# The routing stage of a graph and mixture-of-experts layer: ranks taken one group later on VectorE, scales ahead of picks, one load behind a store

## The chip, the cores and the metric

The kernel runs on one core of one Trainium2 chip. The metric is the device time of one execution in microseconds (us). A core has five engines that run their own instruction streams and meet at semaphores: TensorE (PE, with its weight loads shown as PEld), VectorE (DVE), ScalarE (ACT), GpSimd (POOL) and SyncE (SP), which here only issues DMAs.

## The reference

6250 nodes of 256 features, 100,000 edges, 8 experts of hidden size 1024, two of which are picked per node. Cut to what matters:

```python
xn = _layernorm(x)
x = x + gnn(xn, edges) + mix(xn)              # segment mean over edges, linear attention
# the stage that the change touches prepares this:
xt = _layernorm(x)
logits = xt @ Wr + br                         # 8 logits per node
top_p, top_idx = top_k(softmax(logits), 2)
weights = top_p / top_p.sum(-1)
h = gelu(layernorm_e(xt) @ W1[e] + b1[e]);  y = h @ W2[e] + b2[e]
out = (weights * y[top_idx]).sum(1)
x = x + out
```

## The kernel before

It has three parts in time. The first (0 to 1389 us) does the layer norm, the gather of edges and their sums, and the attention. The second, **routing** (1389 to 1603 us), finds for each node its two experts and its place in each expert's list, and scatters the node's row into a table in DRAM (`bucket_d`) sorted by expert. The third (1603 us to the end) reads that table in expert order and runs the experts.

Each engine has a program written out by hand; instructions of an engine run in the order in which they are written, and semaphores tie the engines together. Nothing is scheduled by a tool.

Routing works on 49 tiles of 128 nodes in 9 groups: groups 0 and 1 have 3 and 4 tiles, the other seven have 6 (`GROUP_LEN`). For each group g the work goes through these steps:

- SP (L562 to L573) loads the two summands of a group (`load_ub`, two DMAs of 768 KB for 6 tiles), waits for `x1_ready` and stores the group's rows to `out` (L567); groups 2 and 3 are loaded ahead of the loop, group g+2 behind the store of group g.
- DVE `r_y` (L1385) adds the first summands; ACT `r_relu` (L919 to L924) takes the relu and the norm; DVE `r_x1` (L1394 to L1410) makes the rows x1 and their mean and variance; ACT `r_sd` (L929) takes the square roots; DVE `r_scale` (L1417 to L1419) makes the scale and bias of the normalised rows and the `ratio` by which the logits are to be scaled.
- ACT `r_pay` (L938) normalises the rows in place, once they are stored (`x1_out`); PE `r_turn` (L1774) transposes them, ACT `r_xT` (L949, L951) copies the transposes out of PSUM, PE `r_logits` (L1785) multiplies by the router's weights.
- DVE `r_pick` (L1426 to L1447) takes the two largest logits and marks them in `oh1`, `oh2` and `picked`. PE `r_rank` (L1795 to L1798) counts, by products with `picked`, how many nodes ahead of each went to the same expert. ACT `r_e2` (L957) takes the exponential for the weights.
- DVE `r_place` (L1454 to L1474) waits for the scatters of group g-2 (they read the same `posi` buffer) and for `rank_mm`, makes the row numbers `posi` and the weights, and signals `pay_ready`.
- POOL `scatters` (L655 to L662) waits for `pay_ready`, then issues two indirect DMAs per tile (L661), 12 for a group of 6. After some groups it also issues one or two plain loads of expert weights (L425).

The orders in the loops are, in turn g: on DVE x1(g), y(g+1), pick(g-1), scale(g), place(g-1); on ACT sd(g), relu(g+1), e2(g-1), pay(g), xT(g); on PE rank(g-1), turn(g), logits(g). The third part starts when all scatters have landed (ACT L975).

The kernel has one buffer each for `rsd`, `ratio` and `nbias`, the outputs of `r_scale`.

Of the kernel before, what the change touches and what calls it, by code (L numbers as in the profile page):

```python
# [10 lines left out]
ALU = mybir.AluOpType  # L11
ACT = mybir.ActivationFunctionType
# [3 lines left out]
P = 128  # L16
# [18 lines left out]
RT = 6  # L35
FIRST, SECOND = 3, 4
GROUP_AT = [0, FIRST] + list(range(FIRST + SECOND, NT, RT))
GROUP_LEN = [FIRST, SECOND] + [RT] * (len(GROUP_AT) - 2)
GROUPS = len(GROUP_AT)
ACCW = D + 2  # L40
HEADS, HD = 4, 32
HID = HEADS * HD
# [3 lines left out]
EXPERTS, HIDDEN = 8, 1024  # L46
# [60 lines left out]
def build_program(nc, x, src, dst, gnn_W, gnn_b, w_qkv, mem_kv, w_out, b_out, g_out, g_pre,  # L107
                  Wr, br, ln_g, ln_b, W1, b1, W2, b2, out):
    ctx = ExitStack()
    with ctx:  # L110
# [214 lines left out]
        def tiny3(*shape):  # L325
            n = 1
            for k in shape:
                n *= k
            k = 0 if used3[0] + n <= D else 1
            used3[k] += n  # L330
            assert used3[k] <= (D, 2 * P * STEPS_J - RT * PAYW)[k]
            v = small3[k][:, used3[k] - n:used3[k]]
            return v.rearrange("p (a b) -> p a b", b=shape[1]) if len(shape) == 2 else v
        rn, nrm, ss6, ratio, nbias, dl, e2, w1, w2 = (tiny3(RT) for _ in range(9))
        ve, sd, rsd = (tiny3(RT, 2) for _ in range(3))
        st6, lg, mx, ix = tiny3(RT, 6), tiny3(RT, 8), tiny3(RT, 8), tiny3(RT, 8)
        mv, ixf, posf = tiny3(RT, 2), tiny3(RT, 2), tiny3(RT, 2)
        posi = [tiny3(RT, 2).bitcast(I32) for _ in range(2)]
# [26 lines left out]
        s = {n: sem(n) for n in names}  # L365
# [73 lines left out]
        def _(sp):  # L439
# [107 lines left out]
            def load_ub(g):  # L547
                u, b = (v[:, 0:GROUP_LEN[g], :] for v in ub_of[g])
                t0, nt = GROUP_AT[g], GROUP_LEN[g]
                sp.dma_start(u, bu_t[:, t0:t0 + nt, D:2 * D]).then_inc(pair["u_in"][g % 2], 16)  # L550
                sp.dma_start(b, bu_t[:, t0:t0 + nt, 0:D]).then_inc(pair["b_in"][g % 2], 16)
# [8 lines left out]


            load_ub(2)  # L562
            load_ub(3)
            for g in range(GROUPS):
                t0, nt = GROUP_AT[g], GROUP_LEN[g]
                sp.wait_ge(s["x1_ready"], g + 1)
                sp.dma_start(out_t[:, t0:t0 + nt, :], acc[:, t0:t0 + nt, 0:D]).then_inc(pair["x1_out"][g % 2], 16)  # L567
                if 2 <= g <= GROUPS - 3:
                    if ub_of[g + 2] is ub_acc:
                        for k in (1, 2):  # L570
                            sp.wait_ge(pair["scattered"][k % 2], scattered_by(k))
                    load_ub(g + 2)
# [4 lines left out]
            for e in range(EXPERTS):  # L577
                r = sp.value_load(padpos_i[0:1, e:e + 1], min_val=0, max_val=PADROW - MT)
# [128 lines left out]
        def _(act):  # L707
            L = Links(act, s["act_links"])
# [92 lines left out]
            for c in range(DC):  # L801
                a = act.activation(w_kv[:, c, :], w_kv[:, c, :], ACT.Copy, scale=gpre[:, c:c + 1])
# [128 lines left out]
            def r_pay(g):  # L931

                t0, nt = GROUP_AT[g], GROUP_LEN[g]
                act.wait_ge(s["scale_ready"], g + 1)
                act.wait_ge(pair["x1_out"][g % 2], 16 * (g // 2 + 1))
                for tt in range(nt):
                    x1 = acc[:, t0 + tt, 0:D]
                    a = act.activation(x1, x1, ACT.Identity, scale=rsd[:, tt, 1:2], bias=nbias[:, tt:tt + 1])  # L938
                    if tt % 3 == 2 or tt == nt - 1:
                        a.then_inc(s["pay_x"], 1)  # L940

# [17 lines left out]
            for g in range(GROUPS):  # L959
                r_sd(g)  # L960
                if g + 1 < GROUPS:
                    r_relu(g + 1)
                if g:
                    r_e2(g - 1)
                r_pay(g)
                r_xT(g)
            r_e2(GROUPS - 1)

# [37 lines left out]
        def _(dve):  # L1006
# [406 lines left out]
            def r_scale(g):  # L1413

                nt = GROUP_LEN[g]
                dve.wait_ge(s["sd_done"], g + 1)
                L.after(dve.reciprocal(rsd[:, 0:nt, :], sd[:, 0:nt, :]))  # L1417
                dve.tensor_tensor(ratio[:, 0:nt].rearrange("p (t o) -> p t o", o=1), sd[:, 0:nt, 1:2], rsd[:, 0:nt, 0:1], ALU.mult)
                dve.scalar_tensor_tensor(out=nbias[:, 0:nt].rearrange("p (t o) -> p t o", o=1), in0=mv[:, 0:nt, 0:1], scalar=-1.0,  # L1419
                                         in1=rsd[:, 0:nt, 1:2], op0=ALU.mult, op1=ALU.mult).then_inc(s["scale_ready"], 1)  # L1420

            def r_pick(g):

                nt, tail = GROUP_LEN[g], g == GROUPS - 1
                dve.wait_ge(s["lg_mm"], g + 1)
                L.after(dve.tensor_tensor(lg[:, 0:nt, :], bank[6][:, 0:nt * EXPERTS].rearrange("p (t e) -> p t e", e=EXPERTS),  # L1426
                                          ratio[:, 0:nt].rearrange("p (t o) -> p t o", o=1).to_broadcast([P, nt, EXPERTS]), ALU.mult))
                L.after(dve.tensor_tensor(lg[:, 0:nt, :], lg[:, 0:nt, :],
                                          br_bc.rearrange("p (o e) -> p o e", o=1).to_broadcast([P, nt, EXPERTS]), ALU.add))
                stand_alone(dve, s["waits_passed"])  # L1430
                for tt in range(nt):
                    a = dve.max(mx[:, tt, :], lg[:, tt, :])
                L.after(a)
                stand_alone(dve, s["waits_passed"])
                for tt in range(nt):
                    a = dve.max_index(ix[:, tt, :].bitcast(U32), mx[:, tt, :], lg[:, tt, :])
                L.after(a)
                L.after(dve.tensor_copy(ixf[:, 0:nt, :], ix[:, 0:nt, 0:2].bitcast(U32)))
                i8 = iota8.rearrange("p (o e) -> p o e", o=1).to_broadcast([P, nt, EXPERTS])
                dve.tensor_tensor(oh1[:, 0:nt, :], i8, ixf[:, 0:nt, 0:1].to_broadcast([P, nt, EXPERTS]), ALU.is_equal)  # L1440
                L.after(dve.tensor_tensor(oh2[:, 0:nt, :], i8, ixf[:, 0:nt, 1:2].to_broadcast([P, nt, EXPERTS]), ALU.is_equal))
                if tail:
                    L.after(dve.memset(picked[:, nt - 1, :], 0.0))
                    L.after(dve.tensor_tensor(picked[0:TAIL, nt - 1, :], oh1[0:TAIL, nt - 1, :], oh2[0:TAIL, nt - 1, :], ALU.add))
                n = nt - 1 if tail else nt
                L.after(dve.tensor_tensor(picked[:, 0:n, :], oh1[:, 0:n, :], oh2[:, 0:n, :], ALU.add))
                dve.tensor_tensor(dl[:, 0:nt], mx[:, 0:nt, 1], mx[:, 0:nt, 0], ALU.subtract).then_inc(s["pick_ready"], 1)  # L1447
# [35 lines left out]
            for g in range(1, GROUPS):  # L1483
                r_x1(g)
                if g + 1 < GROUPS:
                    r_y(g + 1)
                r_pick(g - 1)
                r_scale(g)
                r_place(g - 1)
            r_pick(GROUPS - 1)  # L1490
            r_place(GROUPS - 1)

# [426 lines left out]
```

## Time and profile before

| | us |
|---|---|
| three timed executions | 2305.92, 2300.48, 2290.05 |
| their median | 2300.48 |
| the profiled execution's own time | 2304.02 |
| its span, first to last instruction | 2302.3 |
| mean granted TensorE clock | 0.825 |

The page's busy times over the whole span are PE 1661.6 us (72%), DVE 1304.7 (57%), POOL 1168.1 (51%), ACT 898.4 (39%). They are means over three parts with different limits, so a table by part has to be read before anything is said of routing, which is less than a tenth of the span. A row of the timeline begins with the start and the busy length in us, and ends, in brackets, with the idle time of the engine just before the row and with what ended it; "remote" is a semaphore whose sender the profile doesn't name, "issue" that nothing was waited for that the profile shows.

### The profile page before, as it was taken

What the parts mean: (1) busy time and instruction counts of PE and PEld (TensorE: products, weight loads), DVE (VectorE), ACT (ScalarE), POOL (GpSimd) and SP (SyncE); (2) the same over time, 40 slices, a digit from 0 to 9 for tenths busy, and PEclk for the clock granted to TensorE, in tenths of its full rate; (3) what the DMA queues carried; (4) which work ended last, traced back from release to release, by engine and by line L of the source; (5) the groups of instructions that cost most, each with busy time, mean ns of one, the idle gap of its engine ahead of it and who ended that gap; (6) DMA issues with size and microseconds to landing.
All of it is one profiled execution on the core that took longest, in us unless ns stands there. A gap on an engine that the chain in (4) does not pass through costs nothing. (4 is left out here: it accounts for less than half of the span.)

```text
span 2302.3 us, 34753 instructions
## 1 busy us (share of the span) xinstructions
PE 1661.6 (72%) x9388; PEld 1322.7 (57%) x9389; DVE 1304.7 (57%) x3578; ACT 898.4 (39%) x1839; POOL 1168.1 (51%) x1186
## 2 busy tenths in 40 slices
PE   2856666666656666688666663441999999999997
PEld 1644333444434444334444442441999999999996
DVE  3634333444434566677777667652666666666663
ACT  2801111111101133333444335650666666666663
POOL 0166666666666666656666552664233333333333
PEclk9967776776767888889877776555999999999999
DMA  5333333333333366656656644756456555555554
GB/s 155 124 110 106 102 104 95 103 100 101 97 101 91 120 210 193 200 174 183 211 179 199 190 121 159 253 194 161 107 128 136 129 133 127 136 132 130 131 130 92
DMA packets 195835, 324.99 MB, mean 141 GB/s; under 512 B 33793, under 2 KB 140058, under 8 KB 194711
## 3 DMA queue, kind: packets, MB, share of 16 engines
q0 software_dynamic: 78912, 205.54, 34.4%
q1 hardware_dynamic: 107384, 116.01, 16.3%
q10 hardware_dynamic: 9439, 2.32, 0.5%
q8 instruction: 36, 0.59, 0.1%
q14 instruction: 64, 0.52, 0.1%
HBM read 244.30 MB, written 80.26 MB: 141 GB/s over the span
## 5 line engine op out<-in xcount | busy, mean ns | idle before, releaser
L1225 DVE TENSOR_TENSOR acc_lent<-acc_lent,bank 128x258 f32 x832 | 349.5, 420 | 533.1 <-remote 269.0
L649 POOL DMA_INDIRECT G<-z_d,edge_tabs_lent x416 | 404.2, 972 | 289.0 <-issue 123.1
L649 POOL DMA_INDIRECT w2s_lent<-z_d,edge_tabs_lent x416 | 407.1, 979 | 204.3 <-issue 120.9
L1662 PE MATMUL bank<-G,S_lent 128*128 128x258 f32 x832 | 307.0, 493 | 176.7 <-DVE acc_lent L1225 79.0
L1662 PE MATMUL bank<-w2s_lent 128*128 128x258 f32 x832 | 287.7, 470 | 126.6 <-issue 76.0
L1662 PEld LDWEIGHTS bank<-G,S_lent 128*128 128x128 f32 x832 | 175.8, 239 | 273.4 <-issue 179.5
L1662 PEld LDWEIGHTS bank<-w2s_lent 128*128 128x128 f32 x832 | 167.3, 228 | 212.3 <-issue 144.5
L689 POOL DMA_INDIRECT out_dram<-G,acc_lent x112 | 179.3, 1601 | 205.7 <-DVE G L1550 127.4
L1529 DVE TENSOR_TENSOR acc<-w1s,acc 128x512 fp32r<-128x512 f32 x224 | 154.9, 693 | 217.0 <-ACT acc L975 197.7
L988 ACT ACTIVATE G<-bank,acc_lent 128x256 f32<-128x256 f32 x448 | 188.0, 471 | 193.4 <-DVE acc L1570 82.2
L1858 PE MATMUL bank<-w2s,acc 128*128 x896 | 261.5, 292 | 1.7 <-DVE acc L1570 1.3
L1835 PE MATMUL bank<-acc 128*128 128x256 f32 x896 | 257.8, 288 | 3.3 <-DVE acc L1537 3.3
L1836 PE MATMUL bank<-acc 128*128 128x256 f32 x896 | 253.4, 283 | 0.0
L1837 PE MATMUL bank<-acc 128*128 128x256 f32 x896 | 253.3, 283 | 0.0
L1860 PE MATMUL bank<-w2s,acc 128*128 x896 | 251.6, 281 | 0.0
L849 ACT ACTIVATE w1s<-bank,r 128x256 f32<-128x256 f32 x49 | 23.2, 474 | 523.9 <-remote 269.7
L1835 PEld LDWEIGHTS bank<-acc 128*128 128x128 f32 x896 | 170.4, 190 | 3.8 <-issue 3.8
L1858 PEld LDWEIGHTS bank<-w2s,acc 128*128 128x128 f32 x896 | 169.8, 190 | 2.2 <-issue 2.2
L1837 PEld LDWEIGHTS bank<-acc 128*128 128x128 f32 x896 | 171.0, 191 | 0.0
L1836 PEld LDWEIGHTS bank<-acc 128*128 128x128 f32 x896 | 170.9, 191 | 0.0
L1860 PEld LDWEIGHTS bank<-w2s,acc 128*128 128x128 f32 x896 | 168.3, 188 | 0.0
L1570 DVE TENSOR_TENSOR acc<-G,acc 128x512 fp32r<-128x512 f32 x224 | 154.2, 688 | 8.0 <-ACT acc L998 7.3
(279 smaller groups left out, 3090.1 us busy)
## 6 DMA issues: line engine op xcount, KB each, us to landing
S<-w2lo_d POOLq DMA_DIRECT2D x56, 512.0 KB
edge_tabs<-w2lo_d POOLq DMA_DIRECT2D x56, 512.0 KB
acc_lent<-bucket_d SPq DMA_DIRECT2D x56, 266.0 KB, 2.9
bu_d<-w2s_lent SPq DMA_DIRECT2D x98, 128.0 KB
w2s_lent<-bu_d SPq DMA_DIRECT2D x12, 768.0 KB
w1s<-in_L_ffn_W_dram SPq DMA_DIRECT2D x8, 1024.0 KB
w2s_lent<-in_L_ffn_W_dram SPq DMA_DIRECT2D x32, 256.0 KB
w2hi_d<-w2s_lent SPq DMA_DIRECT2D x32, 256.0 KB
```

The lines of the kernel that those rows point to most:

```text
L649: pool.indirect_dma_start(out=G_half[half][:, k, 0:D], out_offset=None, in_=z_d[:, :], in_offset=bass.IndirectOffsetOnAxis(ap=srcT[:, step ...
L689: pool.indirect_dma_start(out=out[:, :], out_offset=bass.IndirectOffsetOnAxis(ap=nid[par][:, j:j + 1], axis=0), in_=ys[par][:, j, :], in_o ...
L988: g = act.activation(raw[q % 2][:, k * MT:(k + 1) * MT], bank[q][:, k * MT:(k + 1) * MT], ACT.Gelu, bias=b1c[1 - par][:, 2 * q + k:2 * q + ...
L1225: dve.tensor_tensor(to, to, bank[k % 4][:, 0:ACCW], ALU.add).then_inc(s["acc_done"], 1)
L1529: dve.tensor_tensor(w1lo[:, :, cols].bitcast(F32R), w1_part(e, q), w1hi[:, :, cols], ALU.subtract).then_inc(s["w1_ready"], 1)
L1570: dve.tensor_tensor(hlo[:, cols].bitcast(F32R), raw[q % 2], hhi[:, cols], ALU.subtract).then_inc(s["h_split"], 1)
L1662: pe.matmul(bank[k % 4][:, 0:ACCW], S_half[half][:, k // S_GROUP, k % S_GROUP, :], G_half[half][:, k, :], start=True, stop=True).then_inc( ...
L1835: pe.matmul(to, hi, x_hi, start=(k == 0), stop=False)
L1836: pe.matmul(to, hi, x_lo, start=False, stop=False)
L1837: m = pe.matmul(to, lo, x_hi, start=False, stop=(k == DC - 1))
L1858: pe.matmul(to[j], hi, w_hi, start=False, stop=False, skip_group_check=True)
L1860: m = pe.matmul(to[j], lo, w_hi, start=False, stop=(c == HC - 1), skip_group_check=True)
```

## The change

On DVE, turn g of the loop is now x1(g), y(g+1), scale(g), then place(g-2) for groups from 2 on (`DIRECT = 2`), pick(g-1), and place(g-1) only for groups 0 and 1. The last two groups are placed behind the loop: place(7), pick(8), place(8). Since scale(g) now comes ahead of pick(g-1), `ratio`, `nbias` and `rsd` have two buffers each. On ACT, e2(g-1) stands behind pay(g) for g above 2, as before ahead of it for g up to 2. On SP, the load of group 3 is issued behind the store of group 0. The programs of PE and POOL keep their order. A few small tensors lie elsewhere in SBUF.

```diff
+DIRECT = 2
...
-        rn, nrm, ss6, ratio, nbias, dl, e2, w1, w2 = (tiny3(RT) for _ in range(9))
-        ve, sd, rsd = (tiny3(RT, 2) for _ in range(3))
+        rn, nrm, ss6, dl, e2, w1, w2 = (tiny3(RT) for _ in range(7))
+        ratio, nbias = ([tiny3(RT) for _ in range(2)] for _ in range(2))
+        ve, sd = (tiny3(RT, 2) for _ in range(2))
+        rsd = [tiny3(RT, 2) for _ in range(2)]
...
             load_ub(2)
-            load_ub(3)
             for g in range(GROUPS):
                 t0, nt = GROUP_AT[g], GROUP_LEN[g]
                 sp.wait_ge(s["x1_ready"], g + 1)
                 sp.dma_start(out_t[:, t0:t0 + nt, :], acc[:, t0:t0 + nt, 0:D]).then_inc(pair["x1_out"][g % 2], 16)
+                if g == 0:
+                    load_ub(3)
...
                 if g + 1 < GROUPS:
                     r_relu(g + 1)
-                if g:
+                if 0 < g <= DIRECT:
                     r_e2(g - 1)
                 r_pay(g)
+                if g > DIRECT:
+                    r_e2(g - 1)
                 r_xT(g)
...
                 r_x1(g)
                 if g + 1 < GROUPS:
                     r_y(g + 1)
+                r_scale(g)
+                if g - 2 >= DIRECT:
+                    r_place(g - 2)
                 r_pick(g - 1)
-                r_scale(g)
-                r_place(g - 1)
+                if g - 1 < DIRECT:
+                    r_place(g - 1)
+            r_place(GROUPS - 2)
             r_pick(GROUPS - 1)
             r_place(GROUPS - 1)
```

The rows below are the programs' own order, each row one or several equal instructions, with what they wait for in brackets ("dve_links" is DVE's wait for its own last result). Before, DVE has these rows from the end of pick(g-1) over scale(g) to the first rows of place(g-1), here for g = 4:

```order
3186 L1447 TENSOR_TENSOR xTs<-xTs 128x6 [waits dve_links]
3187 L1417 RECIPROCAL xTs<-xTs 128x12 [waits sd_done]
3188 L1418 TENSOR_TENSOR xTs<-xTs 128x6 [waits dve_links]
3189 L1419 SCALAR_TENSOR_TENSOR xTs<-xTs 128x6
3190 L1454 TENSOR_REDUCE dcnt<-picked 128x8 [waits scattered1]
3191 L1456 TENSOR_TENSOR small<-bank,small 128x48 [waits rank_mm]
3192 L1458 TENSOR_TENSOR small<-small 128x48 [waits dve_links]
```

After the change, the same place of a later turn reads as follows: y(g+1) (L1391), scale(g) (L1424 to L1426), then place(g-2) (from L1461), and only behind its last row (L1481) the first of pick(g-1) (L1433):

```order
3240 L1391 SCALAR_TENSOR_TENSOR acc_lent<-acc_lent,rdeg 128x256 [waits u_in1]
3241 L1391 SCALAR_TENSOR_TENSOR acc_lent<-acc_lent,rdeg 128x256 x5
3242 L1424 RECIPROCAL xTs<-xTs 128x12 [waits sd_done]
3243 L1425 TENSOR_TENSOR xTs<-xTs 128x6 [waits dve_links]
3244 L1426 SCALAR_TENSOR_TENSOR xTs<-edge_tabs_lent,xTs 128x6
3245 L1461 TENSOR_REDUCE dcnt<-picked 128x8 [waits scattered0]
3246 L1463 TENSOR_TENSOR small<-bank,small 128x48 [waits rank_mm]
...
3258 L1481 TENSOR_TENSOR acc_lent<-small 128x6x8 [waits dve_links]
3259 L1433 TENSOR_TENSOR xTs<-bank,xTs 128x48 [waits lg_mm,pay_ready]
```

So between a pick and the wait for its ranks there is now a whole x1, y and scale, and the wait for `pay_ready` stands at pick's first row. On ACT, the rows from the norm of one group (L924) to the copies of transposes (L949) were:

```order
736 L924 ACTIVATE xTs<-xTs 128x6 [waits act_links]
737 L957 ACT_TABLE_LOAD
738 L957 ACTIVATE xTs<-xTs 128x6 [waits pick_ready]
739 L938 ACTIVATE acc_lent<-acc_lent,xTs 128x256 [waits x1_out1,scale_ready]
740 L938 ACTIVATE acc_lent<-acc_lent,xTs 128x256 x5
741 L949 ACTIVATE G<-bank 128x256 [waits xT_mm,lg_mm]
```

After the change the normalisation (now L942) comes first, and the table load and the exponential (L961) lie between it and the copies (L953):

```order
736 L928 ACTIVATE xTs<-xTs 128x6 [waits act_links]
737 L942 ACTIVATE acc_lent<-acc_lent,xTs 128x256 [waits x1_out1,scale_ready]
738 L942 ACTIVATE acc_lent<-acc_lent,xTs 128x256 x5
739 L961 ACT_TABLE_LOAD
740 L961 ACTIVATE xTs<-xTs 128x6 [waits pick_ready]
741 L953 ACTIVATE G<-bank 128x256 [waits xT_mm,lg_mm]
```

## Rows read from the trace of the kernel before

**Rows 1.** Table by stretches: engines' busy us (instructions), PEclk, DMA share, GB/s.
```profile
0.00:1389.00 1389.00, 908.59 (x3190) 582.23 (x3191) 748.63 (x2058) 354.86 (x703) 819.46 (x853) 0.79 0.47 140
1389.00:1603.00 214.00, 73.48 (x543) 66.03 (x543) 119.67 (x629) 99.20 (x243) 106.20 (x111) 0.52 0.66 202
1603.00:2302.00 699.00, 679.50 (x5656) 674.45 (x5656) 436.42 (x892) 444.35 (x893) 242.42 (x222) 0.99 0.56 125
```

**Rows 2.** Waits, 1389 to 1640 us: total us, times, longest.
```profile
DVE small L1456 <- remote: 40.7, 6, 10.1
...
ACT acc L975 <- DMA bucket_d<-acc_lent,edge_tabs_lent: 33.6, 1, 33.6
...
POOL bucket_d L661 <- DVE acc_lent L1474: 31.4, 7, 5.3
```

**Rows 3.** POOL timeline: first scatters of groups 2, 4, 5 and 8, group 4's last, the last of all.
```profile
1449.12 1.01 POOL L661 DMA_INDIRECT bucket_d<-acc_lent,edge_tabs_lent  x1 [3.87 <-DVE acc_lent L1474]
...
1490.29 0.97 POOL L661 DMA_INDIRECT bucket_d<-acc_lent,edge_tabs_lent  x1 [5.00 <-DVE acc_lent L1474]
...
1504.47 0.96 POOL L661 DMA_INDIRECT bucket_d<-acc_lent,edge_tabs_lent  x1 [0.30 <-issue]
...
1510.66 1.00 POOL L661 DMA_INDIRECT bucket_d<-acc_lent,edge_tabs_lent  x1 [4.64 <-DVE acc_lent L1474]
...
1571.98 1.01 POOL L661 DMA_INDIRECT bucket_d<-acc_lent,edge_tabs_lent  x1 [4.19 <-DVE acc_lent L1474]
...
1586.61 1.55 POOL L661 DMA_INDIRECT bucket_d<-acc_lent,edge_tabs_lent  x1 [0.30 <-issue]
```

**Rows 4.** DVE timeline: pick(5) begins, place(5) waits for its ranks and ends.
```profile
1497.72 0.20 DVE L1426 TENSOR_TENSOR xTs<-bank,xTs 128x48 f32<-128x48 f32 x1
...
1507.55 0.21 DVE L1456 TENSOR_TENSOR small<-bank,small 128x48 f32<-128x48 f32 x1 [6.09 <-remote]
...
1509.63 0.21 DVE L1474 TENSOR_TENSOR acc_lent<-small 128x48 f32<-128x48 f32 x1
```

**Rows 5.** PE timeline: the last of rank(5), then the transposes of group 6.
```profile
1501.67 0.17 PE L1798 MATMUL bank<-cnt,ones_b 128*128 128x8 bf16 x1
...
1504.50 1.54 PE L1774 MATMUL bank<-ident,acc_lent 128*128 128x128 f32 x6 [2.54 <-issue]
```

**Rows 6.** ACT timeline: pay(6), its transposes copied out, table load for sd.
```profile
1502.88 3.04 ACT L938 ACTIVATE acc_lent<-acc_lent,xTs 128x256 f32<-128x256 f32 x6
1507.69 0.38 ACT L949 ACTIVATE G<-bank 128x256 f32<-128x256 f32 x1 [1.77 <-PE bank L1774]
...
1509.35 1.28 ACT L929 ACT_TABLE_LOAD   x1
```

**Rows 7.** Timelines of PE and DVE: logits(8), and pick(8) released by them.
```profile
1549.69 5.29 PE L1785 MATMUL bank<-Wr_s,G 128*128 128x8 f32 x24 [4.73 <-ACT G L951]
```
```profile
1555.09 0.21 DVE L1426 TENSOR_TENSOR xTs<-bank,xTs 128x48 f32<-128x48 f32 x1 [4.17 <-PE bank L1785]
```

**Rows 8.** The first part, DVE adding what PE summed, and a pause of POOL.
```profile
620.95 0.42 DVE L1225 TENSOR_TENSOR acc_lent<-acc_lent,bank 128x258 f32 x1 [3.78 <-remote]
622.40 0.42 DVE L1225 TENSOR_TENSOR acc_lent<-acc_lent,bank 128x258 f32 x1 [1.03 <-remote]
623.35 0.41 DVE L1225 TENSOR_TENSOR acc_lent<-acc_lent,bank 128x258 f32 x1
```
```profile
623.05 1.19 POOL L649 DMA_INDIRECT w2s_lent<-z_d,edge_tabs_lent  x1 [4.41 <-PE bank L1662]
```

**Rows 9.** Table by stretches, one interval between scatters (group 4's).
```profile
1490.30:1510.70 20.40, 9.57 (x69) 8.63 (x68) 13.25 (x71) 11.97 (x29) 12.40 (x14) 0.50 0.78 248
```

**Rows 10.** The start of routing: SP's first store, ACT's pay(0), DVE's pick(0).
```profile
1395.17 7.59 SPq L567 DMA_DIRECT2D out_dram<-acc_lent  x2
```
```profile
1404.46 1.58 ACT L938 ACTIVATE acc_lent<-acc_lent,xTs 128x256 f32<-128x256 f32 x3 [4.22 <-DMA out_dram<-acc_lent]
```
```profile
1411.43 0.18 DVE L1426 TENSOR_TENSOR xTs<-bank,xTs 128x24 f32<-128x24 f32 x1 [4.46 <-PE bank L1785]
```

More of the change, by code:

```diff
@@ L937, in r_pay @@
                     x1 = acc[:, t0 + tt, 0:D]
-                    a = act.activation(x1, x1, ACT.Identity, scale=rsd[:, tt, 1:2], bias=nbias[:, tt:tt + 1])
+                    a = act.activation(x1, x1, ACT.Identity, scale=rsd[g % 2][:, tt, 1:2], bias=nbias[g % 2][:, tt:tt + 1])
                     if tt % 3 == 2 or tt == nt - 1:
@@ L1416, in r_scale @@
                 dve.wait_ge(s["sd_done"], g + 1)
[L1417 to L1420, printed above, removed]
+                r, bias = rsd[g % 2], nbias[g % 2]
+                L.after(dve.reciprocal(r[:, 0:nt, :], sd[:, 0:nt, :]))
+                dve.tensor_tensor(ratio[g % 2][:, 0:nt].rearrange("p (t o) -> p t o", o=1), sd[:, 0:nt, 1:2], r[:, 0:nt, 0:1], ALU.mult)
+                dve.scalar_tensor_tensor(out=bias[:, 0:nt].rearrange("p (t o) -> p t o", o=1), in0=mv[:, 0:nt, 0:1], scalar=-1.0,
+                                         in1=r[:, 0:nt, 1:2], op0=ALU.mult, op1=ALU.mult).then_inc(s["scale_ready"], 1)
             def r_pick(g):
@@ L1426, in r_pick @@
                 L.after(dve.tensor_tensor(lg[:, 0:nt, :], bank[6][:, 0:nt * EXPERTS].rearrange("p (t e) -> p t e", e=EXPERTS),
-                                          ratio[:, 0:nt].rearrange("p (t o) -> p t o", o=1).to_broadcast([P, nt, EXPERTS]), ALU.mult))
+                                          ratio[g % 2][:, 0:nt].rearrange("p (t o) -> p t o", o=1).to_broadcast([P, nt, EXPERTS]), ALU.mult))
                 L.after(dve.tensor_tensor(lg[:, 0:nt, :], lg[:, 0:nt, :],
```

## The prediction

> **What bounds the kernel now.** I read the table by stretches first [rows 1]. In the third part PE is busy 679.5 of 699 us: nothing in it can give way. The change touches routing alone, 214 us in which no engine is busy for more than 120, so routing is a chain of waits and not a full engine. The table of waits says where the chain runs [rows 2]: DVE stands 40.7 us, in six waits, at L1456, the first instruction of place that reads the ranks, and the third part's first work (ACT L975) waits for the scatters alone. The end of routing is the landing of the last scatter, issued at 1586.61 [rows 3], and what counts is how fast groups of scatters follow each other.
>
> From group 2 (1449.12) to group 8 (1571.98) there are six intervals in 122.86 us, **20.48 us each** [rows 3]. One of them, link by link: the scatters of group 4 are issued from 1490.29 to 1505.43, 15.14 us; 2.12 us later, at 1507.55, DVE gets past L1456 of place(5); place(5) runs to 1509.84, 2.29 us; POOL starts group 5 0.82 us after it, at 1510.66 [rows 3, 4]. 15.14 + 2.12 + 2.29 + 0.82 = 20.37, the measured interval.
>
> Now the odd part. The ranks for which L1456 waits were counted on PE by 1501.84 (1501.67 + 0.17), yet DVE passes at 1507.55, 5.7 us later [rows 4, 5]. In that time POOL was issuing, and DVE passed 2.12 us after it stopped. ACT, waiting for the transposes that PE ran from 1504.50, is released at 1507.69, 0.14 us after DVE [rows 5, 6]. Two waits on PE ending together, behind POOL's last issue, look like one thing holding back PE's semaphores while POOL writes indirect DMAs. The first part shows it too: while POOL issues, DVE gets a sum of PE's only every 4 us or so (3.78 us idle at 620.95), and from POOL's pause at 618.64 (623.05 less 4.41) on they come at 622.40 and quicker after it [rows 8]. Against a complete hold stands logits(8): their record ends at 1554.98, and pick(8) begins at 1555.09, 0.1 us later, while POOL issues too [rows 7]. That release came a few microseconds into a group's scatters, the held ones later in them. I read it as a hold that sets in some 5 to 8 us after POOL starts.
>
> The Trainium skill, Perfetto Trace Analysis, section Tensor Engine Instruction, says that the end of a matmul in a profile is computed, and that its semaphore goes out after PSUM has acknowledged the writes. That allows a gap; no figure is given for it, and that it follows POOL is this trace's own finding.
>
> **The change part by part.** *Place one group later.* Between pick(g) and the wait for its ranks there now are x1, y and scale, some 9 us of DVE's 13.25 busy us per interval [rows 9], and most of a group's scatters. The ranks are then long there, and posi(g) can be ready before POOL has finished group g-1. If nothing else waits, the interval x falls to what POOL needs: 12.40 us busy, one weight load in it, and 11 gaps of 0.30 [rows 3, 9], 15.7, say **15.8 us**, which is 4.7 less than 20.48. DVE fits under it (13.25, and its stalls on its own results), and so do ACT (11.97) and PE (9.57) [rows 9].
>
> *How many intervals gain.* The delay is paid once: place(2) now stands behind x1(4), y(5) and scale(4), about 5.9 + 2.4 + 0.6 = 8.9 us later. Less about 4 us from the start (below) and scale, which stood there before too, scatters(2) begin at about 1453 instead of 1449.12, and scatters(3), 15.8 behind, at about 1469, where they were (1449.12 + 20.48 = 1469.60). So 2 to 3 gives nothing, and 7 to 8 neither: place(8) stands right behind pick(8), as before, and waits for the end of POOL's group. The four intervals from 3 to 7 gain: 4 × (20.48 − x).
>
> *What takes the wait's place.* Taking away DVE's wait doesn't take away what held the semaphore. PE runs rank(g-1), turn(g), logits(g) in that order, and pick(g-1) stands ahead of rank(g-1), so there is a circle that the change leaves whole: pick about 3.3, ranks 0.9, transposes 3.0, release 1.65 (1506.04 to 1507.69) [rows 5, 6], first copies 1.0, logits 5.3 [rows 7]: 15.1 us without any hold. Two semaphores of PE lie in it (transposes, logits). Before, POOL paused some 4 to 5 us in every interval (3.87 to 5.00) [rows 3] and both came out in or near the pause. When POOL hardly pauses, each may be held up to the 4 us that the first part shows [rows 8]. Half of that on average, twice, is 15.1 + 4 = 19.1. I take **x = 19.1** (ends 15.8 and 24.6, the latter below), between the two ends and nearest to the first part, where POOL issues as steadily as it would here. 4 × (20.48 − 19.1) = **5.5 us gained**.
>
> *Scale ahead of pick, two buffers.* scale's three instructions (0.6 us) pass pick's 3.3, so pay(g) may start up to 3.3 us sooner. What it then waits for is the end of relu(g+1), which stands ahead of it on ACT in either order. At the steady state I count it as nothing, within 0 to 0.6 per interval; buffers cost nothing.
>
> *e2 behind pay.* The table load and exponential (1.28 + 0.2) lie in the time in which PE transposes (3.0) and ACT waited 1.77 before the copies [rows 6]: 1.5 of 1.77, so nothing; if that cover is gone, 1.5 us per group in the circle, 4 × 1.5 = 6. e2(g-1) waits for pick(g-1), which now ends later; queued behind it are the copies of group g's transposes, whose PE work itself stands behind rank(g-1), so behind the same pick. That wait costs nothing more.
>
> *The wait for `pay_ready`* moves from x1 to pick; place ends just ahead of either, so nothing.
>
> *SP.* SP's first store was issued at 1395.17 behind four loads of 768 KB, and pay(0) began at 1404.46 after 4.22 us of waiting for it [rows 10]. With two of the loads behind the store it waits less: 0 to 4.2 gained for groups 0 and 1, I take 4. It is not on the path that counts, since scatters(2) now come later for another reason; it is what keeps place(2)'s delay at 4 and not 8. The load of group 3 moves behind that store, some 5 us later, and its first reader y(3) comes 20 us after that.
>
> *DVE beside POOL.* The rule that speaks against the change is in the Trainium skill, SBUF — State Buffer, section SBUF: two separate sides: VectorE and GpSimd share a pair of ports under an exclusive lock, so that descriptors for POOL's DMAs wait while a VectorE instruction of certain kinds holds it. By that rule 2.3 us more of DVE's work per group beside POOL's issuing could lengthen that by as much.
>
> In the rows an issue takes 0.96 us beside DVE's busiest stretch, and the mean of group 4's is (12.40 − 0.59)/12 = 0.98 (a weight load is about 0.59) [rows 3, 9]; the longest row of these is 1.55. With all at 1.55 POOL would need 15.8 + 7 = 22.8. I take nothing.
>
> **Sum.** Against the profiled execution's own 2304.02 us (span 2302.3): −5.5, so about 2298.5. That execution lies 3.5 above the median of the runs shown, 2300.48; against the median it is **2295 us**. All intervals but four, and both other parts, stay as they are.
>
> **The rivals.**
> - *Partly held* (forecast): x from 18 to 20, 2291 to 2299. Chance 0.38.
> - *POOL-bound:* what held the ranks doesn't touch the other semaphores, or they fall early enough in a group, as the logits of group 8 did [rows 7]. x = 15.8 to 17, gain 14 to 19: 2281.5 to 2286. For it: rows 7, and every engine has room. Against: the circle alone is 15.1 and needs DVE to be at pick just then. Chance 0.27.
> - *Nothing gained:* the wait moves whole, from L1456 to the copies of the transposes or to pick, which is then released 2.1 us behind POOL's last issue: x = 20 to 21, 2299 to 2303. For it: ACT was released with DVE in the row shown [rows 6]. Chance 0.2.
> - *Slower, a full hold on the circle:* the transposes come out only when POOL has stopped, and behind them still lie copies 1.65, a table load 1.28 [rows 6], sd 0.2, scale 0.6 and place 2.3, since place(g-2) now stands behind scale(g). With 15.14 + 2.12 before and 0.82 + about 0.4 behind: 15.14 + 2.12 + 1.65 + 1.28 + 0.2 + 0.6 + 2.3 + 1.2 = 24.5. Four intervals at +4.0 to +4.1 are +16: 2317. It decides from the point at which turn(g) is first run later than 5 to 8 us after POOL started, and nothing lets DVE get ahead. Against: POOL would then pause 9 us in each interval, longer than now, in which PE's work of the next turn comes out. The lock on the ports would end near it, at most 4 × (22.8 − 20.48) = +9, 2310. Chance for both 0.15.
>
> **How the numbers follow.** The range: POOL-bound's end less the spread of executions, 2279, to 2312, which leaves out most of the full hold and little else. A change of over 1% (23 us, about what a measurement of this kernel tells from none) lies outside every case: the largest gain worked out is 19, the largest loss 16. So faster 0.06, same 0.88, slower 0.06, the small ones for a front or an end that moves by more than I see.
>
> **What would show it.** Right: L1456's waits (now at the wait of place for its ranks) are gone but for the last group or two; first scatters of groups 3 to 7 stand 19 us apart; new idle time of 2 to 4 us before the copies of transposes or before pick, ended by PE or "remote". POOL-bound: scatters follow without a gap for five groups. Full hold: intervals over 22 us, DVE waiting at scale for sd. Scatters(2) at about 1453 show the delay paid once, pay(0) at about 1400.5 the store. I would be wrong altogether if PE's late semaphores have nothing to do with POOL: then their gap stays the same at any place, is covered by the later place, and the POOL-bound case holds.

## The result

The changed kernel was slower: median 2316.14 us (10 runs, 2309.42 to 2322.66) against 2304.14 us for the kernel before (10 runs), ratio **1.0065, 95% interval 1.0047 to 1.0084**, some 15 us (12 between the medians). The forecast was 2295 us, a gain of 5.5 us, with a range up to 2312. A second measurement (y1, below) gave 1.0074 (1.0047 to 1.0101).

### The profile page after: what moved, and what is told of

The parts are those of the page before. It is cut to its first block and busy times, and to the rows that moved or that the text cites. A ratio compares the mean times of both kernels' runs of the same rounds, so it can differ in the third digit from the quotient of the medians.

```text
span 2314.7 us, 34758 instructions
## 1 busy us (share of the span) xinstructions
PE 1658.3 (72%) x9388; PEld 1324.9 (57%) x9389; DVE 1304.8 (56%) x3578; ACT 898.8 (39%) x1839; POOL 1160.6 (50%) x1186
## 3 DMA queue, kind: packets, MB, share of 16 engines
q1 hardware_dynamic: 107384, 116.01, 16.3%
## 5 line engine op out<-in xcount | busy, mean ns | idle before, releaser
L1673 PE MATMUL bank<-G,S_lent 128*128 128x258 f32 x832 | 295.0, 480 | 142.8 <-issue 71.6
L1673 PEld LDWEIGHTS bank<-G,S_lent 128*128 128x128 f32 x832 | 173.9, 235 | 232.8 <-issue 163.2
L693 POOL DMA_INDIRECT out_dram<-G,acc_lent x112 | 178.7, 1595 | 214.5 <-DVE G L1561 130.7
L853 ACT ACTIVATE w1s<-bank,r 128x256 f32<-128x256 f32 x49 | 23.2, 474 | 516.4 <-remote 337.6
```

The costliest lines, as they stand in the source:

```text
L693: pool.indirect_dma_start(out=out[:, :], out_offset=bass.IndirectOffsetOnAxis(ap=nid[par][:, j:j + 1], axis=0), in_=ys[par][:, j, :], in_o ...
L1673: pe.matmul(bank[k % 4][:, 0:ACCW], S_half[half][:, k // S_GROUP, k % S_GROUP, :], G_half[half][:, k, :], start=True, stop=True).then_inc( ...
```

## The profile after

The first part's code is unchanged, but its length differs from execution to execution (y(0), routing's first work on DVE, began anywhere from 1373.5 to 1402.0 us in the profiles of chips of this kind). So I set y(0) of each profile as zero. Before, it stands at 1389.69; after, here:

```profile
1381.86 0.48 DVE L1391 SCALAR_TENSOR_TENSOR acc_lent<-acc_lent,rdeg,w2s_lent 128x256 f32<-128x256 f32 x1
```

Line numbers of the changed kernel are 4 to 11 higher: scatters are L665, the copies of transposes L953, sd L933, scale's first row L1424, pick's L1433, place's wait for ranks L1463. POOL's timeline, first scatters of groups 2 to 5 and 8:

```profile
1446.52 1.01 POOL L665 DMA_INDIRECT bucket_d<-acc_lent,edge_tabs_lent  x1 [12.23 <-DVE acc_lent L1481]
...
1469.69 1.00 POOL L665 DMA_INDIRECT bucket_d<-acc_lent,edge_tabs_lent  x1 [7.37 <-DVE acc_lent L1481]
...
1492.93 0.96 POOL L665 DMA_INDIRECT bucket_d<-acc_lent,edge_tabs_lent  x1 [8.00 <-DVE acc_lent L1481]
...
1515.36 0.99 POOL L665 DMA_INDIRECT bucket_d<-acc_lent,edge_tabs_lent  x1 [6.60 <-DVE acc_lent L1481]
...
1580.14 1.01 POOL L665 DMA_INDIRECT bucket_d<-acc_lent,edge_tabs_lent  x1 [10.32 <-DVE acc_lent L1481]
```

POOL's idle time ahead of a group was 3.9 to 5.3 us (some of it in [rows 3]) and is now 6.6 to 8.0 ahead of groups 3 to 6. Worked out from these rows and their kind, us from y(0) to a group's first scatter:

| group | 0 | 1 | 2 | 3 | 4 | 5 | 6 | 7 | 8 | end of the last |
|---|---|---|---|---|---|---|---|---|---|---|
| before | 27.6 | 44.5 | 59.4 | 80.1 | 100.6 | 121.0 | 141.6 | 162.0 | 182.3 | 198.5 |
| after | 24.5 | 41.3 | 64.7 | 87.8 | 111.1 | 133.5 | 156.7 | 171.9 | 198.3 | 214.5 |

So routing is 16.0 us longer: scatters(2) come 5.2 us later, the four intervals from 2 to 6 are 23.2, 23.2, 22.4 and 23.2 us instead of 20.4 to 20.6, one is shorter (6 to 7, 15.3) and the last longer (26.4 instead of 20.2). The waits of routing after:

```profile
ACT G L953 <- remote: 54.5, 10, 10.5
POOL bucket_d L665 <- DVE acc_lent L1481: 51.5, 6, 12.2
...
DVE xTs L1424 <- ACT xTs L933: 37.5, 5, 11.2
...
DVE xTs L1433 <- remote: 26.1, 1, 26.1
...
DVE small L1463 <- remote: 3.1, 1, 3.1
```

DVE's 40.7 us of waiting for ranks [rows 2] are down to 3.1, as the change meant. In their place ACT waits 54.5 us for transposes (L953), DVE 37.5 us for sd (L1424), and 26.1 us once for the last logits (L1433). One interval, on ACT and then on DVE, while POOL issues from 1469.69 to 1484.93:

```profile
1482.62 0.38 ACT L953 ACTIVATE G<-bank 128x256 f32<-128x256 f32 x1 [7.94 <-remote]
1482.90 0.59 ACT L955 ACTIVATE G<-bank 128x512 f32<-128x512 f32 x1
1486.81 0.38 ACT L953 ACTIVATE G<-bank 128x256 f32<-128x256 f32 x1 [3.33 <-remote]
1487.09 0.59 ACT L955 ACTIVATE G<-bank 128x512 f32<-128x512 f32 x1
1487.70 1.28 ACT L933 ACT_TABLE_LOAD   x1
1489.00 0.21 ACT L933 ACTIVATE xTs<-xTs 128x12 f32<-128x12 f32 x1
```

```profile
1489.24 0.23 DVE L1424 RECIPROCAL xTs<-xTs 128x12 f32<-128x12 f32 x1 [8.94 <-ACT xTs L933]
...
1489.81 0.20 DVE L1463 TENSOR_TENSOR small<-bank,small 128x48 f32<-128x48 f32 x1
...
1491.90 0.21 DVE L1481 TENSOR_TENSOR acc_lent<-small 128x48 f32<-128x48 f32 x1
```

PE had run the ranks by 1473.0 and these transposes by 1475.8:

```profile
1472.87 0.17 PE L1809 MATMUL bank<-cnt,ones_b 128*128 128x8 bf16 x1
...
1474.34 1.49 PE L1785 MATMUL bank<-ident,acc_lent 128*128 128x128 f32 x6
```

The second half is released at 1486.8, 11.0 us behind its end and 1.9 us behind POOL's last issue; copies, table load, sd, scale and place then stand one behind another, and POOL goes on at 1492.93, 8.0 us after it stopped. The trace also holds the moment of every semaphore's update. Against the end of the matmul that sends it (us later; a few updates are missing from the trace):

```
                        ranks   transposes 1st, 2nd   logits
before, 1481 to 1487    5.5      1.7   0.3             0.01
before, 1501 to 1508    5.7      1.6   0.2             0.01
after, 1473 to 1476     5.2      8.1  11.0             0.01
after, 1496 to 1499     4.4      8.0  10.2             0.01
after, last logits      -        -     -              16.8   (POOL issued from 1538.5 to 1569.8)
POOL silent over 2 us   0.01     0.01  0.01            0.01
```

ACT's and DVE's semaphores show no such lateness: before, the sd that ended at 1495.68, 5.4 us into group 4's issuing, was signalled 0.01 us later, and so were most of their recorded updates in such stretches (0.9 us at most, where the update is there). PE's held ones come out one at a time in the changed kernel's loop, here 4.2 to 4.3 us apart (ranks 1478.25, transposes 1482.53 and 1486.79), in the other groups 2.2 to 5.0.

## The experiments

Theory H: PE's semaphores are held back while POOL issues indirect DMAs. The change moved the ranks and transposes to the beginning of POOL's issuing, and so more of them into the hold. Its rivals were P (the lateness is PE's own), T (the traffic of the DMA engines makes it) and W (the loss comes from DVE's order alone). Each measured ratio below is against the kernel before on the same chip.

**Does POOL's issuing cause it?** Four kernels on one chip. In x1_pause, POOL waits in the middle of a group:

```diff
                 for tt in range(GROUP_LEN[g]):
...
+                    if tt == 4 and 2 <= g <= GROUPS - 2:
+                        pool.wait_ge(s["rank_mm"], g + 2)
```

> The kernel before, with one wait added: POOL stops after the eighth of a group's 12 scatters (groups 2 to 7) until PE's ranks of the next group are out (rank_mm). Theory H, PE's semaphores are held back while POOL issues indirect DMAs and come out 2 to 3 us after it stops: place(g+1) then runs beside the last four issues, DVE's wait at L1456 (40.7 us in six waits) shrinks to under 10 us, intervals between groups fall from 20.5 to 17.5-18.5 us, and the time falls by 6 x 2 to 3 = 12 to 18 us, to 2286 to 2292. Rival P, the lateness belongs to PE alone (a matmul's semaphore comes out when PE has gone on by enough): the pause lasts as long as the wait did, 5 us more per group on top of 15.1, places end no sooner, and the time stays or rises by up to 6 x 4.5 = 27 us.

Measured: ratio 0.9988 (0.9963 to 1.0013), no difference. The pause itself did as H has it: with POOL stopped, ranks came out 0.01 to 0.06 us behind their end in four of six groups, and DVE's waits for them fell from 40.7 to 10.7 us. The gain was not: intervals were 17.8, 18.4, 22.3, 18.4, 16.6 and 23.1 us. The pause freed one semaphore, and the twelve unbroken issues from it to the next pause held another, the logits, for which DVE now waited 24.7 us in three waits. The expectation priced one wait and forgot the other. P's expectation allowed an unchanged time, so the time decides nothing; ranks that are punctual as soon as POOL stands still speak against P.

x2_follow16 puts 16 dummy products behind the ranks instead of one, so that PE goes on working:

> The kernel before, with 16 dummy products (128x128) behind each group's ranks where there was one. Theory H: the ranks are released no sooner, 1.8 to 2.2 us behind POOL's last issue; waits at L1456 stay about 40 us in all; PE gains about 16 x 0.11 = 2 us of work per group, hidden; time within 1% of before. Rival P (the semaphore comes out once PE has enough work behind it): the ranks are out within 3 us of their record's end, the waits fall to under 10 us in all and intervals to 16-17 us, time 2278 to 2285.

DVE's wait for ranks in it, all groups:

```profile
  remote: 41.1, 6
```

The waits are what they were, intervals 20.2 to 20.6 us. Its one execution took 2322.3 us, within the 2301.6 to 2322.5 of the kernel before on that chip. More work of PE behind the ranks doesn't bring them out, so P in this form is out.

x3_late_scatters issues the scatters of groups 3 to 8 only when all are placed:

```diff
-        posi = [tiny3(RT, 2).bitcast(I32) for _ in range(2)]
+        posi = [tiny3(RT, 2).bitcast(I32) for _ in range(8)]
...
-                pool.wait_ge(s["pay_ready"], g + 1)
+                pool.wait_ge(s["pay_ready"], g + 1 if g < 3 else GROUPS)
...
```

> The kernel before, with the scatters of groups 3 to 8 held back until all nine groups are placed (own row-number buffers for each), so that POOL issues nothing while groups 4 to 8 go through the routing. The end is later by design (66 scatters at 1.27 us behind the last place). Theory H: no wait of DVE at L1456 over 1 us from group 4 on, the ranks' semaphore within 1 us of their record's end, and places follow each other every 14.5 to 16.5 us instead of 20.5. Rival P: waits at L1456 of 4 to 6 us stay, places 19 to 20.5 us apart.

DVE reads the ranks in groups 4 to 8:

```profile
1484.33 0.21 DVE L1458 TENSOR_TENSOR small<-bank,small 128x48 f32<-128x48 f32 x1 [0.41 <-PE bank L1800]
...
1499.02 0.21 DVE L1458 TENSOR_TENSOR small<-bank,small 128x48 f32<-128x48 f32 x1 [0.41 <-PE bank L1800]
...
1513.75 0.21 DVE L1458 TENSOR_TENSOR small<-bank,small 128x48 f32<-128x48 f32 x1 [0.41 <-PE bank L1800]
```

They are 14.7 us apart (the later ones 15.0 and 13.9), each wait 0.4 us, each semaphore 0.01 us behind its matmul. Group 3's, run beside the scatters of group 2, was 4.96 us late in the same execution. PE's program is that of before, so the lateness isn't PE's own. In x4_late_and_stores SP adds the traffic of the scatters (12 stores of their size per group):

> As the run with late scatters, and for groups 3 to 8 SP issues 12 plain stores per group of the scatters' size (128 rows of 266 floats, 136 KB) to an unused table, so that the DMA engines carry the scatters' traffic without POOL. Theory H (POOL's issuing holds the semaphores): as the run with late scatters, no wait at L1456 over 1 us. Rival T (the DMA engines' traffic holds them, whoever issues it): waits of 3 to 6 us at L1456 come back, places about 19 to 20 us apart.

Same picture from group 4 on: 13.9 to 15.0 us apart, waits of 0.42 us (0.83 in the last), semaphores 0.01 to 0.02 us late. From 1470 to 1510 the DMA engines moved 282 and then 268 GB/s (20 us each) in x4, 201 and 248 in the kernel before, so T is out for traffic of this size; the stores' rows lie one behind another, where the scatters' are spread over the table, and that difference wasn't tested.

**Is it indirect DMAs or any that POOL issues?** The kernel of x3 with 20 plain DMAs of the same size issued by POOL per group. It ran four times, and only the last, z5, fell on a chip that holds (the others are of the quick kind told of below, and their ranks were 0.01 to 0.02 us late throughout):

> As the run with late scatters, and POOL issues 20 plain DMAs (128 rows of 266 floats to an unused table) per group from group 3 on in their place, so that it issues nearly as long without any indirect DMA. If any DMA that POOL issues holds PE's semaphores: waits of 3 to 10 us for ranks (L1456 in the kernel before) come back in most groups. If only indirect ones do: waits stay under 1 us and places 14.5 to 16 us apart.

> x10_late_pool_plain once more, since that run fell on the chip where nothing is held. On a chip of 2300 us: if any DMA that POOL issues holds PE's semaphores, waits of 3 to 10 us for ranks come back in groups 4 to 8; if only indirect ones do, waits stay under 1 us and places 14.5 to 16 us apart, as in x3_late_scatters. On a chip of 2094 us it says nothing.

> The run with plain DMAs from POOL, a third time, for a chip of 2300 us. If any DMA that POOL issues holds PE's semaphores: waits of 3 to 10 us for ranks in groups 4 to 8, places 18 us apart or more. If only indirect ones do: waits under 1 us and places 14.5 to 16 us apart, as in x3_late_scatters.

> As z4_late_pool_plain, for a chip of 2300 us: with a hold by any DMA of POOL's, waits of 3 to 10 us for ranks in groups 4 to 8; with a hold by indirect ones alone, waits under 1 us and places 14.5 to 16 us apart.

POOL's plain issues in z5, and ACT's copies of transposes that PE ran beside them:

```profile
1541.94 10.86 POOL L680 DMA_DIRECT2D dump_d<-G  x20 [4.37 <-DVE acc_lent L1484]
```

```profile
1542.09 0.38 ACT L959 ACTIVATE G<-bank 128x256 f32<-128x256 f32 x1 [0.22 <-PE bank L1784]
1543.51 0.38 ACT L959 ACTIVATE G<-bank 128x256 f32<-128x256 f32 x1 [0.54 <-PE bank L1784]
```

Ten semaphores of PE (six of transposes, four of logits) were sent while POOL issued plain DMAs, each 0.01 us late; the ranks sent beside the indirect scatters of group 2 in the same execution were 5.75 us late. That speaks for the indirect ones, with a weaker test than the number ten suggests. The six transposes were sent 0.05 to 3.0 us after POOL had begun, where indirect DMAs held none either, and no ranks were sent while it issued. What tells the two apart are three logits, 6.7 to 8.2 us in, and the last ranks, which ended 0.5 us after POOL's last plain DMA and were on time (beside indirect ones transposes that ended 0.2 us after the last were 1.7 us late). With the gaps between indirect issues filled:

```diff
                         pool.indirect_dma_start(...)
+                        iota_f(gap[:, (2 * t + c) * 3:(2 * t + c + 1) * 3], [[1, 3]], 0, 0)
```

> The kernel before with a short iota (about 0.14 us) on POOL behind each indirect scatter, so that the gap between two issues grows from 0.30 to about 0.5-0.6 us. If the hold needs an unbroken row of issues and a short gap lets semaphores out: waits at L1456 go under 10 us in all and intervals are POOL's, 17 to 18.5 us. If it is POOL's issuing as such, however spaced at this scale: waits for ranks stay near 40 us and intervals grow by 12 x 0.2 = 2 to 3 us to 22.5-23.5.

Neither side held. An issue and its gap took 1.31 us instead of 1.27 (the iota of 0.15 us ran inside the old gap), so the longer gap that the run was made for hardly came about. Ranks were 4.2 to 8.0 us late, DVE waited 36.8 us for them, and intervals were 20.4, 20.4, 18.9, 19.1, 20.2 and 17.3. Its one execution of 2287.84 us can't be told from the kernel before (2295.93 there, 2288 to 2310).

**Is it the later place that lost the time?** x7_place_next is the changed kernel with every place right behind its pick again (`DIRECT = 9`, and the call behind the loop left out):

> The changed kernel with every place(g-1) right behind pick(g-1) again: what is left of the change is the load behind the store, scale ahead of pick with two buffers. If the lateness of places is the whole loss: intervals 20.5 us, DVE's waits for ranks 40 us in all as before, the first scatters 3 us sooner after y(0) than before, and the time 0 to 4 us below the kernel before. Rival (scale ahead of pick or the load's new place costs by itself): 3 us or more above the kernel before.

Ratio 0.9994 (0.9973 to 1.0016). Its first scatters stand at 24.4, 41.3, 56.8, 77.2 and the last group's at 178.4 us from y(0), so 2.6 to 3.9 us ahead of before throughout, with intervals of 20.1 to 20.4 from group 2 on, and DVE waits 40.8 us for ranks again. What the load's new place gives is seen in the profile and too small for the measured time. The loss is gone, so it came with the later place or with e2 behind pay: `DIRECT` steers both, and in x7 e2 too stands ahead of pay in every group. No run has e2 moved alone. In the changed kernel's trace its table load and exponential end at 1474.67 and ACT then waits 7.94 us for the transposes, so e2 is covered there, and the later place is left.

x6_place_before_scale takes scale's wait for sd out of POOL's way:

```diff
-                r_scale(g)
                 if g - 2 >= DIRECT:
                     r_place(g - 2)
+                r_scale(g)
```

> The changed kernel with place(g-2) ahead of scale(g) on DVE, nothing else. In the changed kernel scale(g) waits for ACT's sd(g), which stands on ACT behind the held copies of the transposes, and place, thus POOL's next scatters, stands behind scale. If that order is what turned the held semaphores into lost time: POOL gets its next group before scale's wait, its idle time before a group's first scatter falls from 6.6-8 us to under 2, intervals to 16-18 us, and the time comes out 15 to 25 us below the changed kernel (2290 to 2300). Rival: the circle pick, ranks, transposes, logits is itself paced by held semaphores (four per group, 4.2 us each, 16.8, plus work that can't overlap): intervals stay at 21 to 23 us and the time within 5 us of the changed kernel.

Ratio 1.0087 (1.0057 to 1.0117), the changed kernel's loss again, but by neither expectation: intervals of 16.5, 32.2, 16.3, 30.0, 15.3 and 26.3 us. POOL got two groups in a row, and then the logits were held through both:

```profile
1527.57 0.21 DVE L1433 TENSOR_TENSOR xTs<-bank,xTs 128x48 f32<-128x48 f32 x1 [11.17 <-remote]
...
1573.76 0.21 DVE L1433 TENSOR_TENSOR xTs<-bank,xTs 128x48 f32<-128x48 f32 x1 [26.04 <-remote]
```

In both of these orders of DVE the kernel that let POOL issue longer paid for it at the next semaphore of PE.

**Pauses on the changed kernel.** x5_xT_pause:

```diff
+                    if tt == 3 and 2 <= g <= GROUPS - 3:
+                        pool.wait_ge(s["xT_mm"], part(g + 2, 1))
+                    if tt == 2 and g == GROUPS - 2:
+                        pool.wait_ge(s["lg_mm"], GROUPS)
```

> The changed kernel with waits added on POOL: in groups 2 to 6 it stops after the sixth of 12 scatters until the transposes of group g+2 are out (xT_mm), and in group 7 after the fourth until the last logits are out (lg_mm). Theory S (while POOL issues, PE's semaphores come out one at a time, each about 4.2 us behind the one before; a pause lets them out in 1 to 2 us): the copies no longer wait 8 us, intervals fall from 23.2 us to 17-18.5, the wait of 26 us at the last pick shrinks below 8, and the time falls to 15 to 25 us below the changed kernel, that is 3 to 12 us below the kernel before. Rival W (the loss of the changed kernel comes from DVE's longer way to the first scatter and from new waits that have nothing to do with POOL): intervals stay at 22 to 24 us and the pauses add 1 to 2 us each, so 10 us above the changed kernel.

Ratio **0.9953 (0.9925 to 0.9981)**, faster than both kernels. The pauses are 1.5 to 1.7 us long, one 3.1; two of them:

```profile
1452.51 0.96 POOL L669 DMA_INDIRECT bucket_d<-acc_lent,edge_tabs_lent  x1 [1.59 <-remote]
...
1470.22 0.95 POOL L669 DMA_INDIRECT bucket_d<-acc_lent,edge_tabs_lent  x1 [1.70 <-remote]
```

Intervals are 17.4, 17.1, 19.3, 17.7, 16.4 and 21.0 us, and routing ends at 189.5 us from y(0), 25 us ahead of the changed kernel and 9 ahead of before. W is out: it had expected intervals of 22 to 24 us. One wait of 16.3 us for the last ranks stayed, for which the next kernel adds a second pause in group 7 (`if tt == 4 and g == GROUPS - 2: pool.wait_ge(s["rank_mm"], GROUPS)`). It ran twice:

> As x5_xT_pause, and in group 7 POOL stops once more, after the eighth scatter, until the last ranks are out (rank_mm of group 8). In x5_xT_pause place(8) waited 16.3 us for them, until POOL had issued all of group 7. Theory S (a pause lets PE's semaphores out in 1 to 2 us): that wait goes below 3 us, the last interval falls from 21.0 to 16-18.5 us, and the time is 2.5 to 5 us below x5_xT_pause's, 0.6 to 0.8% below the kernel before. Rival: the last interval is bound by something else (pick(8), place(8) themselves): it stays at 20 to 21 us and the time is that of x5_xT_pause, 0.5% below before.

> As x9_two_tail_pauses, which fell on the chip where nothing is held (ratio 1.0014). On a chip with the hold, theory S: the last interval falls from 21.0 to 16-18.5 us, ratio 0.990 to 0.995. On one without: within 0.2% of the kernel before again.

On the chip with the hold (y3) the last interval fell to 18.7 us and that wait to 10.7 us, routing ended at 187.8 us, ratio 0.9957 (0.9932 to 0.9982), where 0.990 to 0.995 was expected. The 1.7 us of routing are less than its interval can show against x5; the wait was expected under 3 us and is 10.7, as it also spans the issues ahead of the pause, so theory S priced it too low. On the other chip (x9) the ratio was 1.0014 (0.9996 to 1.0031), which needs the next point.

**Chips differ.** The chip of x9 took 2094.53 us for the kernel before, not 2300. Both kernels were profiled on a chip of either kind:

> The changed kernel once more, unedited, beside the kernel before on the same chip. The last two runs came from a chip on which the kernel before takes 2094 us and PE's semaphores seem not to be held while POOL issues. If this is such a chip: no hold, the five intervals are POOL's (15.5 to 16.5 us), and the changed kernel is the faster one where the intervals before are longer than that, or equal (2085 to 2097). If it is a chip of 2300 us: ratio 1.005 to 1.009 as first measured, intervals of 22 to 24 us.

> The kernel before, unedited, for its profile on the same chip. On a chip without the hold: no wait of 4 us or more for the ranks (L1456), places 15 to 17 us apart. On a chip with it: six waits, 40 us in all, places 20.5 us apart.

> The changed kernel, unedited, beside the kernel before. On a chip of 2300 us: ratio 1.005 to 1.009, as twice before. On a chip of 2094 us: no hold, so intervals of 15.5 to 16.5 us and a ratio of 0.990 to 1.002, since the delay of one place is paid once (5 us) against at most 1 to 4 us gained in each of four intervals.

> The kernel before, unedited, for its profile. On a chip of 2094 us: no wait for ranks over 1 us, and intervals of 15.5 to 17.5 us, set by DVE's 13.3 us of work and its waits for PE. On a chip of 2300 us: as the first profile, six waits, 40 us.

| | kernel before, us | ratio of the changed kernel | routing, y(0) to last scatter: before, after |
|---|---|---|---|
| chip of y1, y2 | 2299.94 | 1.0074 (1.0047 to 1.0101) | 197.5, 214.1 |
| chip of z2, z3 | 2095.90 | 1.0018 (1.0000 to 1.0036) | 171.2, 174.9 |

In z3, the kernel before on the quick chip, DVE's waits for ranks are these, where [rows 2] have 40.7 us in six:

```profile
  PE bank L1798: 2.8, 6
```

Ranks, transposes and logits are all 0.01 us late there, POOL issuing or not, and intervals are 15.3 to 17.2 us in z3 and 15.3 to 16.6 in z2. So the hold goes with the chip: four different ones showed it (that of x1 to x4, of x5 to x8, of y1 to y3 and of z5; the first two profiles show it too), three did not (x9 and x10, z1 to z3, z4). It costs the unchanged first part far more than routing. DVE's adding of PE's sums in y2, with the hold, and in z3, without:

```profile
L1225 DVE TENSOR_TENSOR acc_lent<-acc_lent,bank 128x258 f32 x832 | 349.5, 420 | 540.2 <-remote 261.0 <-PE bank L1662 173.9 <-issue 71.9
```

```profile
L1225 DVE TENSOR_TENSOR acc_lent<-acc_lent,bank 128x258 f32 x832 | 350.1, 421 | 339.8 <-PE bank L1662 297.8 <-DVE acc_lent L1225 41.1 <-issue 0.5
```

The busy time is the same. The 261.0 us "remote" are gone, part of them is now waiting for PE in the usual way (297.8 instead of 173.9), and DVE's idle time ahead of these rows is 200 us less in all (339.8 instead of 540.2). In y2 a third of the recorded updates behind these sums come over 1 us late, in z3 none over 0.02. y(0) begins at 1203.83 instead of 1390.54 us, 187 of the 204 us between the chips. The granted clock of the first part differs too, 0.79 in y2 and 0.89 in z3, and its share of the 187 us wasn't separated; in routing it is 0.52 in both, so the 26 us there (197.5 against 171.2) are not the clock's. Even without the hold the change doesn't pay: scatters(2) stand 5.0 us later (62.2 against 57.2 from y(0)), as its one delay, and the intervals behind it win back 1.3 us, since before they were at POOL's pace already.

## Why the prediction was wrong

- **What bounds routing:** right. The chain of scatters, ranks' wait and place is as told, and the reading that POOL's issuing holds PE's semaphores was borne out by x3 (gone without scatters), x4 and x2 (neither SP's stores bring it nor more work of PE lifts it) and, more weakly, z5.
- **"I read it as a hold that sets in some 5 to 8 us after POOL starts": this step failed.** In the changed kernel the ranks end at 1473.03, 3.3 us after POOL's first issue at 1469.69, and are held 5.2 us. The logits on which I had leaned ended 3.2 us after it (1554.98 against 1551.74) [rows 7] and were punctual. So a hold can set in at just over 3 us, and the changed order puts ranks and both halves of the transposes behind that point in every group from 3 to 7. Nor is it a matter of time alone: logits that ended 4.25 us (x2) and 4.61 us (x8) after POOL's first issue of a group, and 5.4 and 5.7 us in the first groups of the changed kernel, were 0.01 us late. What decides which semaphore is held stays open.
- **The circle's term was mis-sized.** I took two held semaphores, transposes and logits, at 2 us each. In the loop the logits were on time (0.01 us). Held were three others ahead of the copies' end, ranks and two halves, that come out one behind another, here 4.2 us apart; the last one, 11.0 us late, falls behind POOL's last issue. The 15.1 "without any hold" was wrong too: its release of 1.65 us is itself a held semaphore (1.6 in the table above), so the circle is 13.5 without one. So the interval is not 15.1 + 4 = 19.1 but POOL's 15.24 (1469.69 to 1484.93) + 1.86 to the release (1486.79) + 0.9 copies + 1.3 table load + 0.2 sd + 2.9 for scale and place (1489.24 to 1492.11) + 0.8 = 23.2, as measured. This is the rival called a full hold, priced at 24.5 with a chance of 0.15 for it and the ports together. Its point of decision was the failed step above; its argument against, that PE's work would come out in POOL's long pause, was right for the logits alone: the pause came, 8.0 us of the 9, but the next ranks and transposes ended after POOL had started again.
- **"2 to 3 gives nothing, and 7 to 8 neither":** wrong by two terms. The delay of scatters(2) is 5.2 us (I had 4), but its cost was to be absorbed by a short interval behind it, which was 23.2 us. And 7 to 8 grew from 20.2 to 26.4, because groups 6 and 7 run unbroken and the last logits are held 16.8 us. Sum: +5.2, four intervals +2.5, +2.7, +2.1 and +2.6, then −5.2 and +6.1, together 16.0.
- **e2 behind pay, the moved wait, two buffers:** no cost seen in the trace, as said (e2 lies in ACT's wait of 7.94 us). x7 has scale's place and the buffers without a loss; no run tests e2 alone. **SP:** pay(0) began 11.1 us after y(0) instead of 14.8, so 3.7 gained where I took 4, and it brought nothing measurable (x7).
- **DVE beside POOL:** an issue took 0.96 us in the median and 1.57 at most, before and after. The rival of the ports added nothing.
- **The execution's own sum:** the span grew by 12.4 us: first part −7.8 (code unchanged), routing +16.0, the way from the last scatter to PE's first work for the experts +2.6, experts +1.6. The last two vary as much between profiles of kernels that are alike there (11.5 to 20.5 and 699.4 to 702.4), so only the routing is the change's.

## What to carry to other kernels

Taking away a wait is worth nothing until it is known what made its semaphore late: if the sender is held, ask which semaphore it holds next, and on which path that one stands. Where a single row shows a threshold, look for the nearest case on its other side before resting a term on it. Short deliberate stops, mostly of 1.5 to 1.7 us, in the engine that holds the other were worth more here than the reorderings tried around it, and a measurement on one chip may show the chip: compare the same kernel on several before a gain of half a per cent is believed.

## What the runs showed of the hardware

On the chips of about 2300 us, PE's semaphores can come late while POOL issues indirect DMAs back to back, about 0.96 us each with 0.30 between: ranks by 2.3 to 9.3 us and transposes by up to 11.0 in the two kernels, the changed kernel's last logits by 16.8. In x6, where POOL issues two groups in a row, DVE waited 26 us for the last logits. Not all are late: logits that ended 3.2 us after POOL's first issue were on time. Once POOL stopped issuing them, those still held came out 0.4 (y3) to 3.8 us (the changed kernel) later. SP's stores of the same traffic (0.01 to 0.02 us late) didn't bring it, more work behind PE's last matmul (ranks 5 to 9 us late, unchanged) didn't lift it, and POOL's plain DMAs (0.01 us late, with the few cases named at z5) didn't bring it. ACT's and DVE's semaphores were on time.

On the chips of about 2095 us every recorded update of ranks, transposes and logits was 0.01 to 0.02 us late. What in the chip does this, and why some have it, stays open, as does what decides which semaphore is held and why the last logits of the changed kernel got no turn for 16.8 us where ranks and transposes got one every 2.2 to 5.0 us. A time between two issues of about 0.34 instead of 0.30 us doesn't end it (x8); the shortest stop that did was 1.3 us (y3), and shorter ones weren't tried.
